# A Mamba block and two windowed-attention layers on one core: packed step products, token shift by transfers, queries rotated on GpSimd, another set-up order

## Chip, cores and metric

The kernel runs on one core of a Trainium2 chip. The metric is device time in microseconds (us) of one execution. Lower is better. Three runs of the kernel before gave a median of 1104.92 us (1102.85 to 1107.98).

## What is computed

The input is 16 sequences of 256 tokens with 128 features. First comes a Mamba block with a layer norm, then two layers of local attention and a gated feed-forward network (FFN), then a second layer norm. Cut to what matters here:

```python
u = silu(causal_conv4(x @ in_w + in_b))                # 256 channels
delta = softplus((u @ dt1_w + dt1_b) @ dt2_w + dt2_b)  # rank 16 in between
h = exp(delta*A)*h + (exp(delta*A)-1)/A * B * u        # 16 states, scan over time
y = (C.h + D*u) * silu(x @ gate_w + gate_b)
x = layernorm(x + y @ out_w + out_b)
x0 = x                                                 # then, for each of 2 layers
q, k, v = split(shift_token(x) @ wqkv)                 # 8 heads of 64
q, k = rotary_xpos(l2norm(q)*qs, l2norm(k)*ks)
x = x + local_attention(8*q, k, v) @ wo                # windows of 64, own and one before
h = layernorm(shift_token(x))*ln_g + ln_b              # shift: features 64.. come from the token before
a, g = split(h @ w1 + b1);  x = x + (a*gelu(g)) @ w2 + b2
out = layernorm(x0 + x)                                # after both layers
```

## The kernel before

Everything is float32, but for the mask. The 16 sequences form ten groups of one or two sequences (`SIZES`, line 27). A group goes through the Mamba block as a whole; `f` numbers the 20 pairs of layer and group (`QUAD`, line 81), and `q` the 64 tiles of 128 tokens within them (`TILE`, line 83). Each engine runs one list of steps written out by hand (`PE_ORDER` to `SP_ORDER`, lines 86 to 357), and `run` issues them in that order; semaphores join the engines. An engine so waits at the head of its list, and all behind it waits too. The groups of the Mamba block run interleaved with the attention and FFN of groups before them.

The steps that matter here:

- **Mamba, group g.** TensorE `rank` (two products of 128 rows x 16 columns over all tokens of the group), ScalarE `rank` (adds the bias), TensorE `step_in` (two products of 17 rows x 128 columns, the 17th row of the input being ones for the bias), ScalarE `softplus` (absolute value, exp, ln), VectorE `step_size` (delta). Then for each of 16 states: ScalarE `decay`, VectorE `scan` (line 1073, both inputs in SBUF), TensorE `state_y` (four quadrants of 64 x 64).
- **Attention, tile q.** TensorE `qk_in` fills both AA banks. ScalarE `squares` and VectorE `sums` give the sums of squares (`ss`), GpSimd `scale` turns them into inverse norms (`rn`: line 756, then a power, line 761). VectorE `rope` (lines 1147 and 1148) multiplies queries and keys by the two rotary tables, into `qkc` and `qks`. For keys GpSimd `rotate` adds the two (line 780) and multiplies by the norm (line 783) into `kr`. For queries TensorE does the sum: `qk_T` transposes `qkc` and `qks` into the same bank (line 1407), and transposes `kr` (line 1413): 24 transposes a tile. The queries' norm is left to the softmax: VectorE `row_max`, GpSimd `exp_bias` (line 774: maximum times norm, `nbias`), ScalarE `softmax` (line 926: eight exponentials with a per-partition bias and scale). GpSimd `inverse` (line 767) gives the inverse row sums.
- **FFN, f.** VectorE `attn_sum` (x2), TensorE `shift`: products of x2 with the identity, a shift matrix and a carry matrix into bank M, five products for every two tiles; VectorE `ffn_stats` and `ffn_norm` read bank M. GpSimd `residual` waits for `ffn_norm`. M stays held until `ffn_norm` is done (`HELD`).
- **Set-up.** ScalarE's queue issues ten loads before the first activation, VectorE clears buffers, convolves group 0, makes the coefficients, casts the mask and scales the rotary tables (`masks`, `rotation_tables`), and only then starts its list.

TensorE's products go through the helper at line 1257; a float32 product shows as two instructions in the trace, a transpose as one.

## Time and profile before

| | |
|---|---|
| median of three runs | 1104.92 us |
| the profiled execution | 1106.03 us, its span 1103.8 us |
| TensorE matmul busy | 967.1 us (88%) |
| VectorE busy | 863.2 us (78%) |
| ScalarE busy | 832.3 us (75%) |
| GpSimd busy | 671.5 us (61%) |
| chain that ended last | PE 47%, ACT 18%, issue 13%, DVE 11%, POOL 11% |

Engine names in the profile: PE is TensorE (PEld its weight loads), DVE VectorE, ACT ScalarE, POOL GpSimd, SP the engine that issues transfers. Busy time is the union of an engine's instructions. A group's busy time is the union of that group's alone, and consecutive matmuls overlap in the records, so groups that alternate add up to more than the engine spends; for what a stretch of TensorE work really takes, the chain is the view to read.

### The profile page before, as it was taken

The numbers are of one execution on the slowest core, as the hardware profiler recorded it, in microseconds if no ns is written. First come the engines' busy times: TensorE is split into PE (matmuls) and PEld (weight loads), VectorE is DVE, ScalarE is ACT, GpSimd is POOL, SyncE is SP. The second block draws the span as 40 slices with busy tenths as digits, with TensorE's granted clock in tenths as the row PEclk, the third lists the DMA queues.
The fourth block names the chain that finished last, engine by engine and source line by source line (L and its number), as shares of the span: only waits on it lengthen the run. The fifth ranks groups of instructions, "written<-read, shape, count | busy, mean of one in ns | idle before, by whom it ended". The sixth has DMA issues, their size and how long they took to land.

```text
span 1103.8 us, 27452 instructions
## 1 busy us (share of the span) xinstructions
PE 967.1 (88%) x10784; PEld 593.9 (54%) x10784; DVE 863.2 (78%) x1184; ACT 832.3 (75%) x1909; POOL 671.5 (61%) x513
## 2 busy tenths in 40 slices
PE   4677779799999899999999999998999999996775
PEld 1222345456555465557465646465665766665463
DVE  7776897898888877998799878996988875642543
ACT  4455777886998669886988699877879887783570
POOL 2004764688578666876567857685656777661561
PEclk9988899899999999999999999999999999998897
DMA  6000100000000100000000110010001011010010
GB/s 217 10 15 1 26 1 15 14 18 15 16 16 17 39 20 16 21 16 19 22 17 16 35 26 15 12 40 10 21 7 30 16 25 26 7 25 6 14 32 10
DMA packets 22354, 25.59 MB, mean 23 GB/s; under 512 B 2710, under 2 KB 14545, under 8 KB 22225
## 3 DMA queue, kind: packets, MB, share of 16 engines
q1 hardware_dynamic: 20783, 22.49, 7.9%
q8 instruction: 86, 1.41, 0.5%
q10 hardware_dynamic: 1442, 1.34, 0.4%
q14 instruction: 43, 0.35, 0.1%
HBM read 9.13 MB, written 2.10 MB: 10 GB/s over the span
## 4 chain that ended last, share of the span: by engine, by line
PE 47%; ACT 18%; issue 13%; DVE 11%; POOL 11%; ACTq 1%; POOLq 0%; DVEq 0%
PE M L1257 11%; PE YY L1257 10%; ACT prob L926 8%; PE AA L1257 8%; PE C L1257 6%; DVE scan L1073 4%; PE BB L1257 4%; POOL rn L761 4%; PE BB L1407 2%; PE BB L1395 2%; POOL rden L767 2%; PE C L1458 1%; ACT qkT L914 1%; ACT probT L895 1%; POOL kr L780 1%
## 5 line engine op out<-in xcount | busy, mean ns | idle before, releaser
L1073 DVE TENSOR_TENSOR_SCAN scan<-du,decay 128x1028 f32<-128x1028 f32 (+1 forms) x160 | 297.4, 1898 | 8.7 <-PE YY L1257 4.9
L926 ACT ACTIVATE prob<-BB,nbias,rn 128x128 f32<-128x128 f32 x472 | 208.7, 464 | 48.0 <-POOL nbias L774 47.3
L761 POOL TENSOR_TENSOR rn<-ssc,expo 128x16 f32<-128x16 f32 x64 | 212.5, 3321 | 19.8 <-ACT prob L926 15.1
L871 ACT ACTIVATE decay<-delta,negA 128x1024 f32<-128x1024 f32 (+1 forms) x160 | 153.3, 985 | 16.6 <-DVE scan L1073 12.1
L767 POOL TENSOR_TENSOR rden<-den,minus 128x8 f32<-128x8 f32 x64 | 126.5, 1976 | 49.5 <-ACT prob L926 49.5
L1257 PE MATMUL YY<-scan,diag 64*64 64x512 f32 (+1 forms) x1280 | 142.7, 538 | 15.3 <-DVE scan L1073 15.2
L1257 PE MATMUL AA<-wqkv,hT 128*128 128x512 f32 x256 | 131.4, 638 | 11.8 <-DVE qks L1148 10.2
L756 POOL TENSOR_SCALAR ssc<-ss 128x16 f32<-128x16 f32 x64 | 47.7, 745 | 91.1 <-DVE ss L1130 90.2
L1130 DVE TENSOR_REDUCE ss<-sq 128x16 f32<-128x1024 f32 x64 | 77.3, 1208 | 29.4 <-ACT sq L889 29.3
L926 ACT ACTIVATION_READ_ACCUMULATOR prob<-BB,nbias,rn 128x1 f32 x472 | 99.8, 211 | 0.0
L1162 DVE TENSOR_REDUCE nmax<-BB 128x8 f32<-128x1024 f32 x59 | 71.9, 1218 | 31.8 <-PE BB L1257 31.6
L889 ACT ACTIVATE sq<-AA 128x512 f32<-128x512 f32 x128 | 71.3, 605 | 22.7 <-PE AA L1257 22.5
L780 POOL TENSOR_TENSOR kr<-qkc,qks 128x512 f32<-128x512 f32 x64 | 84.7, 1323 | 5.9 <-DVE qks L1148 5.9
L914 ACT ACTIVATE qkT<-BB 128x512 f32<-128x512 f32 x118 | 64.2, 599 | 26.3 <-PE BB L1413 26.1
L1147 DVE TENSOR_TENSOR qkc<-AA,rope_c 128x1024 f32<-128x1024 f32 x64 | 77.7, 1214 | 5.2 <-PE AA L1257 2.4
L783 POOL TENSOR_TENSOR kr<-kr,rn 128x512 f32<-128x512 f32 x64 | 77.5, 1211 | 5.0
L1257 PEld LDWEIGHTS AA<-wqkv,hT 128*128 128x128 f32 x256 | 46.6, 199 | 62.7 <-issue 61.6
L1257 PE MATMUL M<-hnT,w 128*128 128x512 f32 (+3 forms) x160 | 71.9, 531 | 8.6 <-ACT hid L952 5.1
L1257 PEld LDWEIGHTS C<-v_even,probT 128*64 128x64 f32 x1024 | 64.5, 138 | 26.9 <-issue 18.7
L1148 DVE TENSOR_TENSOR qks<-AA,rope_s 128x1024 f32<-128x1024 f32 x64 | 77.6, 1213 | 0.0
L895 ACT ACTIVATE probT<-BB 128x1024 f32<-128x1024 f32 x59 | 60.8, 1030 | 22.2 <-PE BB L1395 20.9
L1257 PE MATMUL C<-v_even,probT 128*64 128x64 f32 x1024 | 73.1, 225 | 4.1 <-ACT v_odd L905 2.2
(158 smaller groups left out, 2062.4 us busy)
## 6 DMA issues: line engine op xcount, KB each, us to landing
v_even<-v_odd SPq DMA_DIRECT2D x96, 128.0 KB, 2.3
x<-in_x SPq DMA_DIRECT2D x6, 256.0 KB, 3.8
wqkv<-in_wqkv SPq DMA_DIRECT2D x1, 1536.0 KB
xT<-in_xT SPq DMA_DIRECT2D x6, 256.0 KB, 3.8
out<-outb SPq DMA_DIRECT2D x6, 256.0 KB, 2.6
w<-in_w SPq DMA_DIRECT2D x1, 682.0 KB
xT<-in_xT SPq DMA_DIRECT2D x4, 128.0 KB, 2.6
x<-in_x SPq DMA_DIRECT2D x4, 128.0 KB, 4.4
```

Source lines behind the costliest of these rows:

```text
L761: pool.tensor_tensor(rn[:, q % 2, :], ssc[:, :], expo[:, 0:2 * HEADS], ALU.pow).then_inc(rn_sb, 1)
L767: pool.tensor_tensor(rden[:, q % 2, :], den[:, q % 2, :], minus[:, :], ALU.pow).then_inc(rden_sb, 1)
L780: pool.tensor_tensor(kr[:, :], qkc[:, q % 2, 1, :], qks[:, q % 2, 1, :], ALU.add).then_inc(rope_add, 1)
L783: pool.tensor_tensor(heads(kr[:, :]), heads(kr[:, :]), rn[:, q % 2, HEADS:].unsqueeze(2).to_broadcast((P, HEADS, DH)), ALU.mult).then_inc( ...
L871: act.activation(decay[:, at % A_RING, both(g), 1:], delta[:, both(g), :], ACT.Exp, scale=negA[:, n:n + 1]).then_inc(decay_sb, 1)
L914: act.activation(qkT[:, :, :, lo:lo + WIN], bank_of(q, r)[:, :].rearrange("p (a c x) -> p a c x", a=2, c=PAIRS), ACT.Copy).then_inc(qkT_sb, 1)
L926: ins = act.activation(prob[:, h, :], bank_of(q, a)[:, c * P:(c + 1) * P], ACT.Exp, bias=nbias[:, q % 2, h:h + 1], scale=rn[:, q % 2, h:h ...
L1073: dve.tensor_tensor_scan(state, step, a, 0.0, ALU.add, ALU.mult).then_inc(scan_sb, 1)
L1130: dve.tensor_reduce(ss[:, :], sq[:, :, :].rearrange("p a (h x) -> p (a h) x", x=DH), AX.X, ALU.add).then_inc(ss_sb, 1)
L1147: dve.tensor_tensor(dst_c, src, cos, ALU.mult)
L1148: dve.tensor_tensor(dst_s, src[:, :, :, ::-1, :], sin, ALU.mult).then_inc(rope_mul, 2)
L1257: return pe.matmul(dst, lhsT, rhs, start=start, stop=stop, skip_group_check=True)
```

## The change

- **Shift by transfers.** `shift` leaves TensorE's list. SP issues three transfers for each f, from x2 to a new buffer `xs`: the upper half of the features one partition on, the carry row of odd tiles, the lower half as it is. `ffn_stats` and `ffn_norm` read `xs`; `residual` waits for the transfers.
- **Packed step products.** `rank` becomes four products of 32 columns each, one for each half of the channels and half of the tokens, in four column strips; the two halves of the channels are not summed but kept as rows, which `step_in` sums, with 64 rows, two row halves side by side into the two banks. ScalarE's step covers 128 partitions and half the columns; the absolute value is one instruction instead of two.
- **Queries as keys.** `rotate` works on queries and keys at once, in place in `qkc` (1024 elements a partition instead of 512). `qk_T` waits for it and does 16 transposes. `exp_bias` is gone; the exponentials take the negated maximum as bias and no scale.
- **Set-up.** Most loads move from ScalarE's queue to SP's, in another order, A_log alone comes first; the coefficients come ahead of the convolution, `masks` and `tables` become steps of VectorE's list (`masks 0` first of all; `tables 0` after `differences 1`), and three clearings move to GpSimd.
- **All five lists are written anew**, with other distances between the steps.

```diff
+masks 0, differences 0, step_size 0, scan 0 0, scan 0 1, scan 0 2, scan 0 3, scan 0 4, scan 0 5, scan 0 6,
+scan 0 7, scan 0 8, scan 0 9, scan 0 10, scan 0 11, scan 0 12, scan 0 13, scan 0 14, scan 0 15, gated 0,
+mamba_sum 0, conv0 1, conv1 1, mamba_norm 0, differences 1, tables 0, step_size 1, scan 1 0, scan 1 1, scan 1 2,
...
+load_xT 1, load_xT 2, v_even 0, v_even 1, load_xT 3, shift 0, v_even 2, v_even 3, shift 1, v_even 4, v_even 5,
+v_even 6, v_even 7, v_even 8, v_even 9, v_even 10, shift 2, load_xT 4, v_even 11, v_even 12, shift 3, v_even 13,
+v_even 14, shift 4, store 0, v_even 15, v_even 16, load_x 4, v_even 17, v_even 18, load_xT 5, shift 5, v_even 19,
...
+shift 18, store 7, shift 19, store 8, store 9"""
...
             load_xT(0)
+            sp.dma_start(pv[:, :], t["pv"]).then_inc(w_cols, 16)
             sp.dma_start(gate_w[:, :], t["gate_w"]).then_inc(w_gate, 16)
+            sp.dma_start(dt1_w[:, :, :], t["dt1_w"].rearrange("(h p) r -> p h r", h=HALF)).then_inc(w_step, 16)
...
+            sp.dma_start(bv[:, NST:], t["bv"][NST:].partition_broadcast(P)).then_inc(w_rows, 16)
             for g in range(X_RING):
                 load_x(g)
+            for dst, src in [(prob[:, 0:4, :], t["mask"]), (rope_c[:, 0], t["rope_c"]), (rope_s[:, 0], t["rope_s"]),
+                             (rope_c[:, 1], t["rope_c"]), (rope_s[:, 1], t["rope_s"])]:
+                sp.dma_start(dst, src).then_inc(w_rope, 16)
...
+            def shift(f):
+
+                n, mid = tiles_of(QUAD[f][1]), D // 2
+                sp.wait_ge(x2_sb, f + 1)
+                if f:
+                    sp.wait_ge(hn_sb, f)
+                else:
+                    sp.wait_ge(zeros_late, 1)
+                sp.dma_start(xs[1:P, 0:n, mid:], x2[0:P - 1, 0:n, mid:]).then_inc(sh_in, 16)
+                sp.dma_start(xs[0:1, 1:n:2, mid:], x2[P - 1:P, 0:n:2, mid:]).then_inc(sh_in, 16)
+                sp.dma_start(xs[:, 0:n, 0:mid], x2[:, 0:n, 0:mid]).then_inc(sh_in, 16)
...
+            pool.memset(qkT[:, :, :, 0:WIN], 0.0)
+            pool.memset(xs[0:1, :, :], 0.0)
+            pool.memset(v_even[:, :, :], 0.0).then_inc(zeros_late, 1)
...
-                    pool.wait_ge(prob_sb, 2 * (q - 1))
...
-            def exp_bias(q):
-                if q >= 2:
-                    pool.wait_ge(prob_sb, 2 * (q - 1))
-                pool.wait_ge(rn_sb, q + 1)
-                pool.wait_ge(max_sb, q + 1)
-                pool.tensor_tensor(nbias[:, q % 2, :], nmax[:, q % 2, :], rn[:, q % 2, 0:HEADS], ALU.mult).then_inc(nmax_sb, 1)
-
             def rotate(q):
                 pool.wait_ge(rope_mul, 2 * q + 2)
-                if q:
-                    pool.wait_ge(qkT_ps, 2 * q)
-                pool.tensor_tensor(kr[:, :], qkc[:, q % 2, 1, :], qks[:, q % 2, 1, :], ALU.add).then_inc(rope_add, 1)
+                both_qk = qkc[:, q % 2].rearrange("p a x -> p (a x)")
+                pool.tensor_tensor(both_qk, both_qk, qks[:, q % 2].rearrange("p a x -> p (a x)"), ALU.add).then_inc(rope_add, 1)
                 pool.wait_ge(rope_add, q + 1)
                 pool.wait_ge(rn_sb, q + 1)
-                pool.tensor_tensor(heads(kr[:, :]), heads(kr[:, :]),
-                                   rn[:, q % 2, HEADS:].unsqueeze(2).to_broadcast((P, HEADS, DH)),
+                all_heads = heads(both_qk)
+                pool.tensor_tensor(all_heads, all_heads, rn[:, q % 2, :].unsqueeze(2).to_broadcast((P, 2 * HEADS, DH)),
                                    ALU.mult).then_inc(qk_sb, 1)
...
             def residual(f):
                 l, g = QUAD[f]
-                pool.wait_ge(hn_sb, f + 1)
+                pool.wait_ge(sh_in, SHIFT * (f + 1))
                 rows = x2[:, 0:tiles_of(g), :]
...
+            act.dma_start(in_w[:, :], t["in_w"]).then_inc(w_first, 16)
+            act.dma_start(bv[:, 0:NST], t["bv"][0:NST].partition_broadcast(P)).then_inc(w_rates, 16)
+            load_table(EXP_AND_LN)
+            act.wait_ge(w_rates, 16)
+            act.activation(negA[:, :], bv[:, BV["A_log"]:BV["A_log"] + NST], ACT.Exp).then_inc(a_exp, 1)
+            load_table(SILU)
             act.wait_ge(zeros_ready, 1)
-            act.activation(tack[:, :], zero[:, :], ACT.Exp)
...
-                act.activation(dt1_s[0:RANK, 0:tok_of(g)], Y[0][0:RANK, 0:tok_of(g)], ACT.Identity, bias=col("dt1_b", 0, RANK)).then_inc(d1_sb, 1)
+                n = tok_of(g) // 2
+                act.wait_ge(d1_ps, 2 * HALF * (g + 1))
+                act.activation(dt1_s[:, 0:n], Y[0][:, 0:n], ACT.Identity, bias=col("dt1_b")).then_inc(d1_sb, 1)
...
-                    act.activation(th[:, ab(g, h), :], seqs(bk(Y[h], g)), ACT.Abs).then_inc(za_sb, 1)
-                act.wait_ge(za_sb, HALF * g + HALF)
+                act.wait_ge(z_ps, 2 * HALF * (g + 1))
+                act.activation(by_half(th[:, both(g), :]), z_of(g), ACT.Abs).then_inc(za_sb, 1)
+                act.wait_ge(za_sb, g + 1)
                 act.activation(th[:, both(g), :], th[:, both(g), :], ACT.Exp, scale=-1.0).then_inc(e_sb, 1)
...
-                act.wait_ge(nmax_sb, q + 1)
...
                         h = 2 * c + a
                         ins = act.activation(prob[:, h, :], bank_of(q, a)[:, c * P:(c + 1) * P], ACT.Exp,
-                                             bias=nbias[:, q % 2, h:h + 1], scale=rn[:, q % 2, h:h + 1],
+                                             bias=nmax[:, q % 2, h:h + 1],
                                              accum_out=den[:, q % 2, h:h + 1])
...
-            dve.memset(qkT[:, :, :, 0:WIN], 0.0)
-            dve.memset(v_even[:, :, :], 0.0).then_inc(zeros_ready, 1)
-            dve.wait_ge(w_first, F_W)
+            dve.memset(upre[:, :, 0:TAPS - 1], 0.0).then_inc(zeros_ready, 1)
...
+            def state_weights():
+
+                dve.wait_ge(w_cols, 16)
...
                 dve.engine_nop().then_inc(coeff_done, 1)
 
-            def masks():
+            def masks(_):
                 dve.wait_ge(w_rope, R_W)
                 dve.wait_ge(w_mamba, M_W)
                 dve.tensor_copy(identb[:, :], ident[:, :])
                 dve.tensor_copy(mask[:, :, :, :].rearrange("p j w x -> p (j w) x"), prob[:, 0:4, :]).then_inc(mask_done, 1)
...
-                for h in range(HALF):
-                    ins = dve.scalar_tensor_tensor(out=delta[:, ab(g, h), :], in0=seqs(bk(Y[h], g)), scalar=0.0,
-                                                   in1=th[:, ab(g, h), :], op0=ALU.max, op1=ALU.add)
+                for k in range(2):
+                    ins = dve.scalar_tensor_tensor(out=by_half(delta[:, both(g), :])[:, :, k], in0=z_of(g)[:, :, k], scalar=0.0,
+                                                   in1=by_half(th[:, both(g), :])[:, :, k], op0=ALU.max, op1=ALU.add)
...
-                    dve.wait_ge(nmax_sb, q - 1)
+                    dve.wait_ge(prob_sb, 2 * (q - 1))
...
+                dve.wait_ge(sh_in, SHIFT * (f + 1))
                 for i in range(tiles_of(g)):
-                    ins = dve.bn_stats(f_st[:, i, :], rows[:, i, :])
+                    ins = dve.bn_stats(f_st[:, i, :], xs[:, i, :])
...
+            coefficients()
+            dve.wait_ge(w_cols, 16)
             convolve(0, 0)
             convolve(0, 1)
-            coefficients()
-            masks()
-            rotation_tables()
+            state_weights()
...
-                for h in range(HALF):
-                    ins = mm(Y[0][0:RANK, 0:tok_of(g)], dt1_w[:, h, :], u[:, ab(g, h), 1:], h == 0, h == HALF - 1)
-                ins.then_inc(d1_ps, 1)
+                n = tok_of(g) // 2
+                for k in range(2):
+                    for h in range(HALF):
+                        lo = (2 * k + h) * PART
+                        if SIZES[g] == 2:
+                            rhs = u[:, h * SIZES[g] + k, 1:]
+                        else:
+                            rhs = u[:, h, 1 + k * n:1 + (k + 1) * n]
+                        mm(Y[0][lo:lo + PART, 0:n], dt1_w[:, h, :], rhs).then_inc(d1_ps, 1)
...
                 for h in range(HALF):
-                    mm(bk(Y[h], g), dt2_w[:, h * P:(h + 1) * P], bk(dt1_s, g)).then_inc(z_ps, 1)
+                    for k in range(2):
+                        mm(Y[k][:, h * n:(h + 1) * n], dt2_w[half(k), h * P:(h + 1) * P], dt1_s[half(k), 0:n]).then_inc(z_ps, 1)
...
-                pe.wait_ge(rope_mul, 2 * q + 2)
-                for part in range(2):
+                pe.wait_ge(qk_sb, q + 1)
+                for a in range(2):
                     for c in range(PAIRS):
                         for w in range(2):
-                            pe.matmul(bank_of(q, w)[:, c * WIN:(c + 1) * WIN], (qkc, qks)[part][half(w), q % 2, 0, c * P:(c + 1) * P],
-                                      ident[half(w), half(w)], start=part == 0 and c == 0, stop=part == 1,
-                                      is_transpose=True, skip_group_check=True)
-                pe.wait_ge(qk_sb, q + 1)
-                for c in range(PAIRS):
-                    for w in range(2):
-                        ins = pe.matmul(bank_of(q, w)[:, (PAIRS + c) * WIN:(PAIRS + c + 1) * WIN],
-                                        kr[half(w), c * P:(c + 1) * P], ident[half(w), half(w)], start=False, stop=True,
-                                        is_transpose=True, skip_group_check=True)
-                        if c == PAIRS - 1:
-                            ins.then_inc(qkT_ps, 1)
+                            ins = pe.transpose(bank_of(q, w)[:, (a * PAIRS + c) * WIN:(a * PAIRS + c + 1) * WIN],
+                                               qkc[half(w), q % 2, a, c * P:(c + 1) * P], ident[half(w), half(w)])
+                            if a and c == PAIRS - 1:
+                                ins.then_inc(qkT_ps, 1)
...
-            def shifted(f):
-                l, g = QUAD[f]
-                pe.wait_ge(x2_sb, f + 1)
-                free("shift", f)
-                for i in range(tiles_of(g)):
-                    lo, mid, hi = i * D, i * D + D // 2, (i + 1) * D
-                    mm(M[:, lo:mid], ident[:, :], x2[:, i, 0:D // 2])
-                    ins = mm(M[:, mid:hi], shift[:, :], x2[:, i, D // 2:], True, i % 2 == 0)
-                    if i % 2:
-                        ins = mm(M[:, mid:hi], carry[:, :], x2[:, i - 1, D // 2:], False, True)
-                ins.then_inc(sh_ps, 1)
...
+    dt1_w[:, :RANK] = m["dt1_w"]
+    dt2_w = np.zeros((P, DI), np.float32)
+    for k in (0, P // 2):
+        dt1_b[k:k + RANK, 0] = m["dt1_b"]
+        dt1_b[k + RANK, 0] = 1.0
+        dt2_w[k:k + RANK] = m["dt2_w"]
+        dt2_w[k + RANK] = m["dt2_b"]
+        dt2_w[k + PART:k + PART + RANK] = m["dt2_w"]
```

## Rows read from the trace of the kernel before

**Rows 1.** Windows: stretch; busy us of PE, PEld, DVE, ACT, POOL; PEclk, DMA share, GB/s.

```profile
200.00:950.00 750.00, 711.27 (x8309) 444.36 (x8306) 636.35 (x822) 623.59 (x1449) 523.34 (x384) 0.99 0.08 20
400.00:500.00 100.00, 96.02 (x1068) 56.66 (x1067) 89.74 (x94) 89.63 (x200) 74.57 (x51) 1.00 0.08 20
1000.00:1050.00 50.00, 37.69 (x290) 22.99 (x289) 21.85 (x36) 20.94 (x47) 19.46 (x17) 0.86 0.07 17
```

**Rows 2.** The chain in order of time (start, us, what), a TensorE-bound part.

```profile
503.95 2.18 PE M L1257 x20
506.13 0.64 PE BB L1407 x16
...
517.14 1.91 PE YY L1257 x4
```

**Rows 3.** Waits: engine, line, releaser, us in total, times, longest.

```profile
ACT prob L926 <- POOL nbias L774: 51.0, 28, 6.7
```

**Rows 4.** Windows of line 783 alone, the middle: its instructions are the tiles.

```profile
200.00:950.00 750.00, 62.76 (x51) 0.99 0.08 20
```

**Rows 5.** Groups by form, ScalarE: busy us, mean ns, idle time before and releaser.

```profile
L871 ACT ACTIVATE decay<-delta,negA 128x1024 f32<-128x1024 f32 x96 | 108.5, 1159 | 2.6 <-DVE scan L1073 1.7 <-DVE delta L1052 0.8
...
L860 ACT ACTIVATE th<-th 128x1024 f32<-128x1024 f32 x6 | 6.3, 1058 | 0.2
```

**Rows 6.** Source lines of GpSimd: ns min/median/max, first and last start.

```profile
L780 POOL TENSOR_TENSOR kr<-qkc,qks x64: 1259/1272/2852, 95.8 to 1057.5; 128x512 f32<-128x512 f32 x64
...
L783 POOL TENSOR_TENSOR kr<-kr,rn x64: 1041/1042/2922, 97.2 to 1058.9; 128x512 f32<-128x512 f32 x64
...
L794 POOL TENSOR_TENSOR x<-x,bv x20: 720/1271/2647, 164.8 to 1087.7; 128x512 f32<-128x512 f32 x12, 128x256 f32<-128x256 f32 x8
```

**Rows 7.** Groups of GpSimd instructions, columns as in rows 5.

```profile
L756 POOL TENSOR_SCALAR ssc<-ss 128x16 f32<-128x16 f32 x64 | 47.7, 745 | 91.1 <-DVE ss L1130 90.2
...
L774 POOL TENSOR_TENSOR nbias<-nmax,rn 128x8 f32<-128x8 f32 x64 | 21.3, 332 | 88.1 <-DVE nmax L1162 83.4 <-ACT prob L926 4.7
...
L734 POOL TENSOR_TENSOR diag<-ident,wsum 128x1088 f32<-128x1088 f32 x2 | 4.2, 2128 | 3.0 <-DVEq L1007 3.0
```

**Rows 8.** Timeline (start, us, engine): three scans and GpSimd beside them.

```profile
487.25 6.67 DVE L1073 TENSOR_TENSOR_SCAN scan<-du,decay 128x1028 f32<-128x1028 f32 x3
...
488.50 5.46 POOL L756 TENSOR_SCALAR ssc<-ss 128x16 f32<-128x16 f32 x1
```

**Rows 9.** Source line of the scan, starts 499 to 618 us: ns min/median/max.

```profile
L1073 DVE TENSOR_TENSOR_SCAN scan<-du,decay x17: 2269/2287/3309, 499.2 to 618.3; 128x1028 f32<-128x1028 f32 x17
```

**Rows 10.** Groups by form, VectorE: columns as in rows 5.

```profile
L1073 DVE TENSOR_TENSOR_SCAN scan<-du,decay 128x1028 f32<-128x1028 f32 x96 | 222.1, 2346 | 3.1 <-PE YY L1257 2.5 <-ACT decay L871 0.5
```

**Rows 11.** Transfers: KB each, median us from issue to landing.

```profile
v_even<-v_odd SPq DMA_DIRECT2D x96, 128.0 KB, 2.3
...
rope_s<-in_rope_s ACTq DMA_DIRECT2D x2, 128.0 KB, 8.2
```

**Rows 12.** Timeline of SP: one issue late in the kernel.

```profile
1056.20 0.46 SPq L708 DMA_DIRECT2D v_even<-v_odd  x1
```

**Rows 13.** Timeline of the set-up, ScalarE and VectorE.

```profile
5.72 1.29 ACTq L814 DMA_DIRECT2D rope_s<-in_rope_s  x1
...
8.44 0.82 ACT L824 ACTIVATE upre<-YY,pv 128x256 f32<-128x256 f32 x2
...
16.72 2.23 DVE L1013 CAST mask<-prob 128x512 bf16<-128x512 f32 x1
...
22.58 0.74 DVE L1052 SCALAR_TENSOR_TENSOR delta<-YY,th 128x256 f32<-128x256 f32 x2
```

**Rows 14.** The chain in order of time: step products of group 1, last shift products.

```profile
52.16 1.90 PE YY L1257 x4
54.60 2.08 PE YY L1257 x4
...
1083.60 1.31 PE M L1257 x10
```

More of the change, by code:

```diff
@@ L171 @@
-shift 18, probs_T 62, weighted 62, norm_T 18, out_T 62, probs_T 63, up_gate 18, weighted 63, up_a 18 0,
-up_a 18 1, up_a 18 2, out_T 63, down 18, attn_out 19, shift 19, norm_T 19, up_gate 19, up_a 19 0, up_a 19 1,
-up_a 19 2, down 19"""
+state_y 1 14, state_y 1 15, mamba_out 1, u_in 2, gate_in 2, rank 2, step_in 2, qk_in 1, layer_T 0 1, qk_T 0,
+scores 0, qk_in 2, qk_T 1, qk_in 3, probs_T 0, scores 1, v_in 2, weighted 0, skip 2, state_y 2 0, state_y 2 1,
+probs_T 1, out_T 0, state_y 2 2, qk_T 2, v_in 3, state_y 2 3, weighted 1, scores 2, state_y 2 4, out_T 1,
@@ new lines @@
+attn_out 0, state_y 2 5, state_y 2 6, probs_T 2, qk_T 3, weighted 2, state_y 2 7, scores 3, state_y 2 8,
+state_y 2 9, state_y 2 10, state_y 2 11, state_y 2 12, norm_T 0, up_gate 0, state_y 2 13, state_y 2 14,
+probs_T 3, state_y 2 15, up_a 0 0, out_T 2, mamba_out 2, weighted 3, u_in 3, up_a 0 1, out_T 3, layer_T 0 2,
+gate_in 3, v_in 4, qk_in 4, rank 3, up_a 0 2, step_in 3, qk_in 5, down 0, attn_out 1, qk_T 4, qk_in 6, scores 4,
+layer_T 1 0, v_in 5, qk_in 7, qk_T 5, skip 3, probs_T 4, v_in 6, scores 5, weighted 4, state_y 3 0, state_y 3 1,
```

584 lines of the change are left out of this document (276 added, 308 removed).

## Prediction

> **What bounds the kernel now.** I read the busy shares by windows first. From 200 to 950 us TensorE is busy 711.3 of 750 us (94.8%), VectorE 636.4, ScalarE 623.6, GpSimd 523.3 [rows 1]. The chain in order of time says the same: long unbroken runs of PE pieces, so there the order of TensorE's own work sets the pace [rows 2]. The ends are different: from 1000 us TensorE is busy 75% of the time at a granted clock of 0.86 [rows 1], and the chain goes from engine to engine, piece by piece; the first 160 us are like that too. Last the waits: ScalarE stands 51 us for `nbias`, which GpSimd makes in list order after VectorE's maximum [rows 3]. So three questions: what TensorE's middle loses in work, what engine is next, and what the ends gain or lose in latency.
>
> **TensorE, the middle.** The 51 tiles of the middle [rows 4] are the unit. The shift products of four tiles take 2.18 us of the chain, 0.55 us a tile: 28 us. (The groups of the page count alternating matmuls twice, so I take chain pieces.) The second eight transposes for queries are half of a 0.64 us piece, 0.32 us a tile: 16 us [rows 2]. The step products: a pair of 512-column products takes 1.91 us [rows 2]; `rank` streams a quarter of the columns if its four strips run side by side, `step_in` half, so about 1.4 and 0.95 us a group, and six groups, one of them small, fall in the middle: 12 us. No row shows four 32-column strips; the bounds are no gain (strips one after the other stream as many columns as now) and the quarter, and between them I take the quarter, since in `state_y` four quadrants already run together. The Trainium skill, "TensorEngine Tiling (Array Packing)", section Theoretical Speedup, gives up to 4x for a dimension of at most 32; by it the sum would be the one I take, 655; by the rows' other end, without overlap in `rank`, 663. Sum: 711 - 56 = 655 us.
>
> **ScalarE.** An activation with a per-partition scale over 1024 elements takes 1159 ns, one with a constant scale 1058 [rows 5]: 101 ns for the scale operand. Eight exponentials a tile lose it: 0.8 us a tile, 41 us in the middle, so 583. Bounds: nothing (the operand's fetch hides behind the neighbour) and 0.1 us each; I take the rows' difference, since it does not depend on the size much. The absolute value as one instruction and the shorter bias step save under 1 us a group.
>
> **GpSimd.** The added addition and product are as wide again. An addition takes 720 ns at 256 elements and 1271 at 512 [rows 6], so 2.37 us at 1024; a product 1041 at 512 [rows 6] and 2128 at 1088 [rows 7], so 2.01 us at 1024. `rotate` goes from 2.30 to 4.38 us, 2.08 us more a tile: 106 us. `exp_bias` gives back 332 ns a tile [rows 7], 17 us. Sum 523 + 106 - 17 = 612 us.
>
> **The two SBUF readers.** A tiny GpSimd instruction, 242 to 255 ns when free, took 5.46 us while VectorE ran three scans back to back, and ended with them [rows 8]; over the kernel its mean is 745 ns [rows 7]. It also goes the other way: a scan beside GpSimd work took 3309 ns instead of 2269 [rows 9], and the mask's cast took 2.23 us while GpSimd made its product of 2.13 us [rows 7, 13]. So scans and GpSimd's reads exclude each other, and the longer `rotate` holds longer. A VectorE instruction that meets it waits for the remainder: chance and remainder both grow with the length, so a loss now of about 76 ns a scan (mean 2346 [rows 10] over the minimum, some 7 us over the kernel) grows by (2.37/1.26)^2 = 3.5; I put 12 us on VectorE's middle (648) and 15 on GpSimd's (627). The Trainium skill, "SBUF — State Buffer", section Who interferes with whom, states it as an exclusive lock: a VectorE instruction with two SBUF inputs and a GpSimd instruction that reads SBUF shut each other out for the whole instruction. By that rule, the trace agrees (5.46 us); it is the rule that speaks against this change, since it moves work from TensorE, which never meets the scans, to the engine that does. The rival below is built on it.
>
> **What the middle comes to.** The four sums are 655, 648, 583 and 627: 2513 us of work where it was 2495. What falls is the peak, not the work. Two ends from rows: if TensorE stays the pace at 94.8%, 655/0.948 = 691 us, 59 less; if the four engines together are kept only as busy as now (3.33 engines on the mean), 2513/3.33 = 755, 5 more. The densest stretch here, 400 to 500 us, keeps 3.50 engines busy [rows 1], which would give 718. I take 720: TensorE at 91%, VectorE at 90, GpSimd at 87, ScalarE at 81. **Middle: 30 us less.** In the new lists `qk_T` stands on the mean 22.0 steps behind its `qk_in` (21.5 before, not counting `shift`), and `norm_T` 15.2 behind `attn_out` (12.3): room was made for the transfers, little for the longer `rotate`, which moves qk_T by 2.1 us in a tile's 14.7.
>
> **The transfers.** Each f issues three. SP's copies inside SBUF land in 2.3 us [rows 11] and an issue takes 0.46 us [rows 12], so the last of three lands 3.2 us after x2 at best, about 4 with 256-byte pieces in the same queue, against 2.18 (four tiles) or 1.31 us (two) of products [rows 2, 14]. In the middle the wider distance covers it; bank M is also free earlier, since nothing holds it from `attn_sum` to `ffn_norm`. Behind a waiting `shift` on SP stand `v_even` copies; `weighted` waits for them; I put nothing on it and up to 0.5 us a tile at the upper end. `residual` now waits for transfers instead of `ffn_norm`, with `inverse` and `scale` behind it: landing comes before the norm, so no cost.
>
> **Set-up and first groups.** ScalarE's first activation stands at 8.44 us, behind ten issues, the last from 5.72 to 7.01 us, and a table load [rows 13]; now about 6.4, when `u_in` is through. From the mask's cast at 16.72 us to delta 0 at 22.58 VectorE does mask and rotary tables [rows 13], 5.9 us; the tables leave that way, as `tables 0` they stand where VectorE waits for ScalarE's softplus anyway. Against it: `masks 0` is first in VectorE's list and waits for the rotary loads, now issued on SP behind some twelve others, at about 8 to 9 us instead of 5.72; landing took 8.2 us [rows 11, 13]. That puts the mask at 14 to 17 us, with `differences 0` and `step_size 0` behind it, and delta 0 at 17 to 19: 5 us earlier (bounds 3 and 7; a price for the clearings moved to GpSimd is inside, since its first real input comes later). Step products of groups 1 and 2 lie on the chain: 1.90 to 0.5, 2.08 to 1.05 [rows 14], 3 us together. The first tiles, still unhidden, pay 2 us for `rotate`. **Set-up: 6 us less.**
>
> **The end.** Last f: 1.31 us of products [rows 14] become 3.4, 2.1 more; the one before it shares its wait with the last tiles, 1 more. Four last tiles pay 2.1 us each on GpSimd; from 1000 to 1050 us it is busy 19.5 of 50 us [rows 1], so most of the 8 us fall into its waits: 2.5 more. Five softmaxes on the chain are 0.8 us shorter and lose a GpSimd hop: 5 less. **End: 1 us more.**
>
> Together -6 - 30 + 1 = -35 us. The profiled execution took 1106.0 us (span 1103.8 and 2.2 around it), 1.1 above the median of the runs; so 1071 for it and **1070** for the median.
>
> **Rivals.**
> 1. *TensorE keeps the pace* at 94.8%: middle 59 less, 1041. For it: 400 to 500 us has TensorE at 96% with two others at 90% [rows 1]. Against: GpSimd would be at 91%, where it was at 75.
> 2. *The relief is eaten.* Four nearly equal engines in fixed lists wait for each other; the middle stays at 3.33 busy engines, 755 us; with the ends 1105. A lower clock would work the same way: the granted clock is 0.99 where TensorE is busy 95% and 0.86 where it is 75% [rows 1], and 91% lies between.
> 3. *Slower: the scans shut GpSimd out.* There are 160 scans for 64 tiles, often in runs of two or three. If `rotate`'s two instructions wait w us more a tile than now, the middle is (627 + 51 w)/0.948; from w = 1.65 it is over 750. With w = 2.2, less than half of the 5.2 us that the tiny instruction lost in rows 8, it is 780: 30 more, 1130. Against it: the mean loss of that instruction is only 0.5 us.
> 4. *The packing doesn't overlap*: 8 us more work on TensorE, 8 us in the middle, 1078; it is inside the forecast's own range.
>
> **Chances.** The forecast with rival 4, 0.52 (1055 to 1088); rival 1, 0.17 (1036 to 1055); rival 2, 0.16 (1088 to 1110); rival 3, 0.15. A measurement of this kernel tells about 0.5% from no change, 5.5 us. Faster by more than that: all of the first two and a third of rival 2, 0.74; the same 0.10; slower 0.16. The range leaves out most of rival 3 and a little below rival 1: 1038 to 1112.
>
> **What would show it.** Right: `rotate`'s instructions at 2.4 and 2.0 us; exponentials near 360 ns; TensorE's busy time near 895 us in all; TensorE and VectorE both near 90% in the middle; delta 0 at 17 to 19 us. Wrong: waits of TensorE for line 783's result in many tiles (rival 3), scans with a mean over 2450 ns, waits of VectorE for `xs`, or a clock under 0.95 in the middle (rival 2).

## The result, and the profile after

The changed kernel takes **1165.9 us** (median of 4 runs, 1157.4 to 1168.1) where the kernel before took 1104.5 (4 runs beside it): ratio 1.054, interval 1.048 to 1.060. It is slower by 61 us; the forecast was 1070 with an upper end of 1112, so even the sign is wrong. The profiled execution took 1168.1 us, with a span of 1166.3 us at a mean granted clock of 0.919 (before 0.967).

The page of the kernel after, busy time and the clock by slices:

```profile
PE 939.5 (81%) x10032; PEld 558.8 (48%) x10032; DVE 881.9 (76%) x1180; ACT 786.0 (67%) x1896; POOL 810.4 (69%) x452
PEclk9897899899989999998989998998999897987985
```

The windows of the kernel after (stretch; busy us of PE, PEld, DVE, ACT, POOL; clock, DMA share, GB/s), to be held against [rows 1]:

```profile
200.00:950.00 750.00, 654.29 (x7258) 390.46 (x7256) 631.87 (x783) 557.32 (x1359) 611.78 (x314) 0.95 0.09 23
400.00:500.00 100.00, 85.34 (x876) 48.28 (x874) 84.12 (x108) 78.23 (x179) 81.15 (x44) 0.97 0.09 22
1000.00:1050.00 50.00, 40.05 (x523) 29.43 (x521) 21.77 (x45) 33.51 (x99) 33.93 (x25) 0.90 0.10 23
```

The work went where it was meant to go: over the kernel TensorE has 28 us less than before (967.1 then), ScalarE 46 less, GpSimd 139 more. But no engine is the bound of the middle any more: TensorE is at 87%, VectorE at 84, GpSimd at 82. The clock has gone from 0.99 to 0.95, and the same 750 us hold 47 tiles where they held 51 [rows 4]; the windows of line 797 alone, the product of `rotate`, one instruction a tile (stretch; GpSimd's busy us in it; clock, DMA share, GB/s):

```profile
200.00:950.00 750.00, 111.14 (x47) 0.95 0.09 23
```

Time is lost in waits. The first view to read for that is SyncE's own timeline (start, us, engine, line):

```profile
520.00 0.74 SPq L726 DMA_DIRECT2D xs<-x  x1
520.78 6.49 SPq L727 DMA_DIRECT2D xs<-x  x1
527.32 0.68 SPq L728 DMA_DIRECT2D xs<-x  x1
528.04 0.62 SPq L667 DMA_DIRECT2D xT<-in_xT  x1
```

and line 727 in all (the issue behind the first transfer; ns min/median/max, first and last start):

```profile
L727 SPq DMA_DIRECT2D xs<-x x20: 2645/6431/6530, 133.6 to 1139.6; - x20
```

Line 726 issues the transfer of partitions 0 to 126. The next issue, of a transfer with two pieces, holds SyncE for 6.4 us where f has four tiles and for 2.65 where it has two; I had reckoned 0.46 us an issue [rows 12]. The chain of the kernel after goes straight through it (start, us, what):

```profile
519.31 0.67 DVE x L1186
520.00 0.74 SPq L726
520.78 6.49 SPq L727
527.32 0.68 SPq L728
528.04 3.45 DMA xT<-in_xT
531.54 3.78 PE YY L1264 x4
```

Here even the load of the next group's xT, with which the shift has nothing to do, stands behind it, and TensorE behind that. The chain of the whole kernel by engines, from its page:

```profile
PE 40%; ACT 15%; DVE 12%; issue 10%; SPq 9%; POOL 5%; DMA 4%; DVEq 0%; POOLq 0%; ACTq 0%
```

SyncE has 9% of it and transfers 4%; in the stretch of [rows 2] neither appears. The waits (engine, line, releaser, us in total, times, longest):

```profile
DVE f_st L1192 <- DMA xs<-x: 79.5, 20, 8.8
PE YY L1264 <- DMA xT<-in_xT: 22.2, 5, 6.6
POOL f_ve L763 <- DVE f_mv L1197: 109.7, 16, 23.3
PE M L1485 <- DVE hn L1206: 29.7, 6, 9.0
```

All twenty `ffn_stats` wait for the transfers, 4 us each, with VectorE's scans queued behind them, and GpSimd's `ffn_rstd`, ScalarE's `norm_T` and TensorE's `norm_T` in a row behind those.

### The profile page after: what moved, and what is told of

Its sections match the earlier page's. It is cut to its first block, busy times and chain, and to the rows that moved or that the text cites. A ratio compares the mean times of both kernels' runs of the same rounds, so it can differ in the third digit from the quotient of the medians.

```text
span 1166.3 us, 25804 instructions
## 1 busy us (share of the span) xinstructions
PE 939.5 (81%) x10032; PEld 558.8 (48%) x10032; DVE 881.9 (76%) x1180; ACT 786.0 (67%) x1896; POOL 810.4 (69%) x452
## 4 chain that ended last, share of the span: by engine, by line
PE 40%; ACT 15%; DVE 12%; issue 10%; SPq 9%; POOL 5%; DMA 4%; DVEq 0%; POOLq 0%; ACTq 0%
PE M L1264 9%; PE YY L1264 8%; PE AA L1264 7%; SPq L727 7%; PE C L1264 7%; DVE scan L1082 4%; ACT prob L934 4%; PE BB L1264 3%; DMA xs<-x 3%; PE BB L1421 2%; PE C L1467 2%; POOL rn L782 2%; PE BB L1409 1%; ACT decay L879 1%; DVE qks L1157 1%
## 5 line engine op out<-in xcount | busy, mean ns | idle before, releaser
L1082 DVE TENSOR_TENSOR_SCAN scan<-du,decay 128x1028 f32<-128x1028 f32 (+1 forms) x160 | 315.9, 2017 | 12.4 <-PE YY L1264 7.8
L782 POOL TENSOR_TENSOR rn<-ssc,expo 128x16 f32<-128x16 f32 x64 | 224.3, 3504 | 5.3
L934 ACT ACTIVATE prob<-BB,nmax 128x128 f32<-128x128 f32 x472 | 166.1, 380 | 51.0 <-DVE nmax L1171 50.6
L793 POOL TENSOR_TENSOR qkc<-qkc,qks 128x1024 f32<-128x1024 f32 x64 | 158.2, 2472 | 5.3 <-DVE qks L1157 5.2
L797 POOL TENSOR_TENSOR qkc<-qkc,rn 128x1024 f32<-128x1024 f32 x64 | 145.3, 2271 | 5.0
L934 ACT ACTIVATION_READ_ACCUMULATOR prob<-BB,nmax 128x1 f32 x472 | 103.9, 220 | 0.0
L763 POOL TENSOR_SCALAR f_ve<-f_mv 128x4 f32<-128x4 f32 (+1 forms) x20 | 11.1, 553 | 110.0 <-DVE f_mv L1197 109.7
L1264 PE MATMUL M<-hnT,w 128*128 128x512 f32 (+3 forms) x160 | 77.5, 569 | 6.4 <-ACT hid L960 4.0
L944 ACT ACTIVATE oT<-C 128x512 f32<-128x512 f32 x64 | 38.7, 605 | 61.2 <-PE C L1467 58.5
L1264 PE MATMUL C<-v_odd,probT 128*64 128x64 f32 x1024 | 78.0, 233 | 0.0
```

The lines of the kernel that those rows point to most:

```text
L782: pool.tensor_tensor(rn[:, q % 2, :], ssc[:, :], expo[:, 0:2 * HEADS], ALU.pow).then_inc(rn_sb, 1)
L793: pool.tensor_tensor(both_qk, both_qk, qks[:, q % 2].rearrange("p a x -> p (a x)"), ALU.add).then_inc(rope_add, 1)
L797: pool.tensor_tensor(all_heads, all_heads, rn[:, q % 2, :].unsqueeze(2).to_broadcast((P, 2 * HEADS, DH)), ALU.mult).then_inc(qk_sb, 1)
L934: ins = act.activation(prob[:, h, :], bank_of(q, a)[:, c * P:(c + 1) * P], ACT.Exp, bias=nmax[:, q % 2, h:h + 1], accum_out=den[:, q % 2, ...
L1082: dve.tensor_tensor_scan(state, step, a, 0.0, ALU.add, ALU.mult).then_inc(scan_sb, 1)
L1264: return pe.matmul(dst, lhsT, rhs, start=start, stop=stop, skip_group_check=True)
```

## The experiments

Every run was timed in three rounds beside the kernel before (medians 1103.8 to 1107.4 us in the four sets); a ratio is always to that. A difference of medians from two sets carries their 3.6 us with it; where it matters, the difference by the ratios stands beside it. "Old order" is the kernel before's lists of steps, "new order" the changed kernel's.

**1. The first transfer in two.** Expected before it ran:

> The changed kernel with one edit: the transfer that moves x2 down by one row (partitions 0-126 to 1-127) is issued as two, of 112 partitions and of 15, so a shift is four transfers. Theory T (the 127-partition transfer is what costs: the second issue of each shift holds SyncE's list 6.4 us for a four-tile f and 2.7 us for a two-tile f, and its bytes land late): every issue of the shift under 1 us, SyncE's share of the chain of waits from 9% to under 3%, VectorE's wait of f_st for the transfer from 79.5 us to under 35 us, TensorE's wait for xT (22.2 us) near nothing; time 1075 to 1110 us. Rival L (lock: GpSimd's rotate of 4.7 us and VectorE's long scans slow each other, mean scan 2524 ns against 2346): the issues get short but the time stays above 1145 us and the scans stay above 2500 ns. Rival O (the new hand-written order is the worse one whatever the transfers cost): above 1140 us with DVE, ACT and PE waiting for each other, not for transfers.

```diff
-sp.dma_start(xs[1:P, 0:n, mid:], x2[0:P - 1, 0:n, mid:]).then_inc(sh_in, 16)
+sp.dma_start(xs[1:CUT + 1, 0:n, mid:], x2[0:CUT, 0:n, mid:]).then_inc(sh_in, 16)
+sp.dma_start(xs[CUT + 1:P, 0:n, mid:], x2[CUT:P - 1, 0:n, mid:]).then_inc(sh_in, 16)
```

(with CUT = 112 and SHIFT = 16 * 4). Measured **1116.3 us**, ratio 1.011 (1.007 to 1.015): the same bytes in one more transfer are 50 us faster (47 by the ratios). The issue behind the first transfer is line 728 of this kernel (ns min/median/max):

```profile
L728 SPq DMA_DIRECT2D xs<-x x20: 911/952/1708, 132.1 to 1088.1; - x20
```

and its waits have for VectorE:

```profile
DVE f_st L1194 <- DMA xs<-x: 31.2, 12, 4.4
```

The wait fell by 48 us, the time by 50. Theory T holds, and lock and order (L and O) are refuted as the cause of these 50 us, since both wanted more than 1140 us. Some of T's numbers missed: 1116 is just above the 1075 to 1110 expected, TensorE's wait for xT fell from 22.2 to 7.3 us and not to nothing, and one issue took 1.7 us. Rival L's other mark, scans over 2500 ns, is nearly met (2498), and the kernel is still 12 us over the kernel before; that is left to experiments 5 to 7.

**2 and 3. The size or the number of partitions?** The same kernel with the cut moved to 126 and to 113:

> split_transfer with the cut at 126: one transfer of 126 partitions and one of a single partition. Theory D (a transfer is spread over as many of the 16 DMA engines as divide its number of partitions, at most 16: 14 for 126, 16 for 112, one for 127): the issues behind it stay under 1.2 us and the time is within 1% of split_transfer, 1105 to 1128 us. Rival S (size or lack of a full set of partitions): near the changed kernel's 1166 us, with an issue of some 6 us.

> split_transfer with the cut at 113, a prime: transfers of 113 and 14 partitions, that is one partition more and one less than in split_transfer. Theory D: the issue behind the first is held 113/127 of 6.4 us for a four-tile f, some 5.7 us, and most of the gain of the split is gone, 1148 to 1168 us. Rival S (the size alone): issues under 1.2 us and 1105 to 1128 us.

```diff
-        CUT = 112
+        CUT = 126
```

and CUT = 113. Measured **1116.5 us** (ratio 1.009, 1.007 to 1.011) for 126 and **1167.5 us** (1.057, 1.052 to 1.061) for 113. The issue behind the first transfer, with 126 partitions in it:

```profile
L728 SPq DMA_DIRECT2D xs<-x x20: 632/663/676, 133.8 to 1089.9; - x20
```

and with 113:

```profile
L728 SPq DMA_DIRECT2D xs<-x x20: 2276/5656/5738, 132.4 to 1140.0; - x20
```

One partition more than 112 costs 51 us; with 126, thirteen more again, they are back. So size is refuted (rival S) and theory D stands. For 113 and 127, both primes, the hold scales with the pieces: 5656/6431 is 0.88, and 113/127 is 0.89. The two sizes of f agree: 508 pieces of 256 bytes hold the issue 3786 ns longer than 254 (6431 against 2645), and 452 hold it 3380 ns longer than 226 (5656 against 2276), 14.9 and 15.0 ns for each piece more. The windows tell how many engines moved the bytes: the last two figures are the mean busy share of the core's 16 DMA engines and GB/s. While the first transfer runs, in the kernel after and in cut_113:

```profile
521.00:527.00 6.00, 4.63 (x40) 3.23 (x38) 1.90 (x4) 4.79 (x20) 5.92 (x4) 1.00 0.07 16
520.50:525.50 5.00, 4.15 (x39) 3.04 (x37) 1.42 (x3) 4.00 (x18) 4.92 (x4) 1.00 0.08 17
```

and in split_transfer (112 partitions, then 15) and cut_126:

```profile
501.10:501.60 0.50, 0.50 (x2) 0.23 (x2) 0.50 (x1) 0.50 (x4) 0.50 (x1) 1.00 0.90 188
502.00:502.20 0.20, 0.20 (x1) 0.00 (x1) 0.20 (x1) 0.20 (x2) 0.20 (x1) 1.00 0.39 72
509.20:509.70 0.50, 0.50 (x2) 0.00 (x1) 0.50 (x2) 0.50 (x4) 0.50 (x2) 1.00 0.88 192
```

A share of 0.07 to 0.08 is little more than one engine of 16, at 16 to 17 GB/s; 0.9 is nearly all of them, at 190. And 15 partitions reach 0.39, over six engines, so it is not that 127 and 113 are odd. That is the rule of the Trainium skill, "DMA: Bandwidth & Descriptors", section Why a DMA increments its semaphore by 16 and not by 1: the number of DMA engines that share a transfer is the largest one up to 16 that divides its slowest dimension, so 16 for 112 or 128 partitions and one for 127; by it 126 has 14 and 113 one. The times agree in all four cases, and the shares with one engine for 127 and 113; 16 for 112 against 14 for 126 is more than shares of 0.90 and 0.88 can tell apart.

**4. Held list or late bytes?** The changed kernel, unsplit, with the three transfers issued the other way round:

> The changed kernel, unsplit, with the three transfers of a shift issued in the opposite order, so that the 127-partition one comes last. Rival H (SyncE's list held 6.4 us is the loss): the first two issues at 0.7 us, what follows is held only where it comes within 6 us, time 1125 to 1145 us. Theory W (what costs is that VectorE waits for the late bytes): f_st's wait stays near 75 us and the time within 1% of the changed kernel's, 1152 to 1178 us.

```diff
-sp.dma_start(xs[1:P, 0:n, mid:], x2[0:P - 1, 0:n, mid:]).then_inc(sh_in, 16)
-sp.dma_start(xs[0:1, 1:n:2, mid:], x2[P - 1:P, 0:n:2, mid:]).then_inc(sh_in, 16)
 sp.dma_start(xs[:, 0:n, 0:mid], x2[:, 0:n, 0:mid]).then_inc(sh_in, 16)
+sp.dma_start(xs[0:1, 1:n:2, mid:], x2[P - 1:P, 0:n:2, mid:]).then_inc(sh_in, 16)
+sp.dma_start(xs[1:P, 0:n, mid:], x2[0:P - 1, 0:n, mid:]).then_inc(sh_in, 16)
```

Measured **1180.6 us** (1.067, 1.066 to 1.069), 15 us worse than the changed kernel and a little over the top of theory W's range. Its timeline of SyncE:

```profile
524.95 0.72 SPq L728 DMA_DIRECT2D xs<-x  x1
525.72 6.41 SPq L667 DMA_DIRECT2D xT<-in_xT  x1
```

and VectorE's wait:

```profile
DVE f_st L1192 <- DMA xs<-x: 95.9, 20, 9.6
```

All three issues of the shift are now quick; the hold moved on to whatever comes next, here the load of xT. That is so behind 15 of the 20 long transfers: the next load or `v_even` copy takes 2.6 to 6.5 us. VectorE's wait grew from 79.5 to 95.9 us, 0.8 us for each of the twenty: the long transfer starts two issues later. Rival H's 1125 to 1145 us did not come, and issuing the long transfer last gains nothing. But the list was not free in this run either, and TensorE still waits 20.4 us for xT (22.2 in the kernel after). So whether the late bytes or the held list make more of the 50 us is not shown; that the wait of `ffn_stats` for the bytes fell by 48 us with the split speaks for the bytes.

**5 to 7. What split transfers and the rotation still cost.** Three kernels on top of split_transfer, in the new order, which leave work out:

> split_transfer with GpSimd's rotation cut to the half of the keys (512 elements a partition in place of 1024), same order, waits and everything else; the queries go on without their sum and their norm, so the output differs from the reference's. It prices the doubled rotation in the new order with nothing given back. Theory G (GpSimd's longer list costs even in the new order): 1065 to 1100 us, against 1116. Rival (the rotation is hidden there, the rest of the gap is TensorE and the transfers): 1108 us or more.

> split_transfer without any shift: ffn_stats and ffn_norm read x2 itself, no transfers, no TensorE; the residual goes to the buffer that the transfers filled. The output differs from the reference's. It gives the time with a shift that costs nothing, so the difference to split_transfer is all that split transfers still cost. Theory T2 (the landing of 3 us plus about 3 us of issues, twenty times, 31 us of f_st's waits, partly hidden): 1085 to 1105 us. Rival (split transfers are free): 1112 us or more.

> split_no_shift and split_half_rotate together (output differs from the reference's). If the two costs are of their own, the gains add; if both wait in one chain it is more or less than the sum. Theory: 1045 to 1080 us, near the forecast's 1070, which counted the transfers and the rotation at nothing. If it stays above 1095 us, what is wrong with the forecast is elsewhere (order, TensorE).

```diff
-both_qk = qkc[:, q % 2].rearrange("p a x -> p (a x)")
-pool.tensor_tensor(both_qk, both_qk, qks[:, q % 2].rearrange("p a x -> p (a x)"), ALU.add).then_inc(rope_add, 1)
+keys = qkc[:, q % 2, 1, :]
+pool.tensor_tensor(keys, keys, qks[:, q % 2, 1, :], ALU.add).then_inc(rope_add, 1)
```

for the half rotation (the product likewise), and for no shift:

```diff
-dve.wait_ge(sh_in, SHIFT * (f + 1))
+dve.wait_ge(x2_sb, f + 1)
-    ins = dve.bn_stats(f_st[:, i, :], xs[:, i, :])
+    ins = dve.bn_stats(f_st[:, i, :], x2[:, i, :])
```

| kernel, new order | us | ratio (interval) |
|---|---|---|
| split_transfer | 1116.3 | 1.011 (1.007 to 1.015) |
| split_half_rotate | 1093.8 | 0.986 (0.981 to 0.990) |
| split_no_shift | 1090.2 | 0.982 (0.978 to 0.985) |
| split_neither | 1064.5 | 0.958 (0.954 to 0.963) |

The half rotation alone gives 23 us, no shift alone 26, both 52 (by the ratios 28, 33 and 58): the two costs add, so neither hides the other. And with both gone the kernel stands at 1064, where the forecast had 1070 with both counted at almost nothing. Its windows:

```profile
200.00:950.00 750.00, 693.97 (x8015) 421.68 (x8006) 653.16 (x854) 608.34 (x1512) 553.69 (x352) 0.98 0.09 21
```

TensorE is at 92.5% and the clock at 0.98, as the forecast drew its middle; GpSimd is at 74%, where the forecast had 87 with the whole rotation. With the half rotation GpSimd's share of the chain falls from 17% (split_transfer) to 8%. Part of the rotation's 23 us may go through VectorE. Groups by form, the wide scans (busy us, mean ns, idle time before) in split_transfer:

```profile
L1084 DVE TENSOR_TENSOR_SCAN scan<-du,decay 128x1028 f32<-128x1028 f32 x96 | 236.5, 2498 | 6.9 <-PE YY L1266 5.7 <-ACT decay L881 1.2
```

and in split_half_rotate:

```profile
L1083 DVE TENSOR_TENSOR_SCAN scan<-du,decay 128x1028 f32<-128x1028 f32 x96 | 225.8, 2387 | 6.8 <-PE YY L1265 6.2 <-ACT decay L880 0.6
```

Scans are 11 us shorter over the kernel, and all of VectorE 23 (886.4 against 863.3), though nothing was edited there; GpSimd itself has 134 us less (806.9 against 673.1). Which of the two carries the 23 us of time these runs can't say.

**8 and 9. Each part alone, in the old order.**

> The kernel before with one part of the change alone: the shift by three transfers in place of TensorE (part_b of the skip product lies in hu's room, so that xs fits), everything else and the order of all other steps as before. Theory T: the whole loss comes from here, 1145 to 1180 us, the second issue at 6.4 us for a four-tile f. Rival L: no more than 1115 us, since rotate is the old one. Rival O: no more than 1115 us, since the order is the old one.

> The kernel before with the other part alone: the sums and norms of queries on GpSimd beside those of keys, 16 transposes a tile in place of 24, exponentials without a scale operand, no exp_bias step; shift on TensorE, order as before. Theory T: within 1.5% of before, 1085 to 1110 us; TensorE's busy time down by about 20 us, exponentials near 380 ns, rotate at 2.4 + 2.2 us. Rival L: slower, 1125 us or more, with scans above 2500 ns. Rival O: as T.

The edits are those of the diff, cut to one part, in the kernel before. Transfers alone, unsplit: **1228.8 us**, 1.113 (1.108 to 1.118), 49 over the top of what T expected. The rotation alone: **1164.1 us**, 1.055 (1.051 to 1.059): T expected no more than 1110, and rival L, 1125 or more, had it right in time. Exponentials (382 ns) and `rotate` (2.49 and 2.21 us) came as T said; TensorE's busy time did not fall by 20 us but rose from 967.1 to 971.5, at a clock of 0.944. The chain of before_plus_rotate by engines:

```profile
POOL 40%; PE 25%; issue 19%; DVE 9%; ACT 5%; ACTq 1%; DMA 0%; POOLq 0%; DVEq 0%; SPq 0%
```

and TensorE's wait for the rotated queries and keys:

```profile
PE BB L1387 <- POOL qkc L764: 41.1, 21, 4.9
```

The chain of the kernel before had 11% GpSimd. Rival L wanted scans over 2500 ns; they are at 2460 here, and 2346 before [rows 10]. So the lock falls short of what L asked of it, and GpSimd's list has the larger part by the chain: with 611 us busy in the middle (81.5%) in an order made for 523, it is what the others wait for. No run separates the two. GpSimd's share had room; the order had none.

**10. All but the transfers, old order.**

> The changed kernel's set-up, packed step products and rotation with the kernel before's shift on TensorE and the kernel before's order of steps. Theory T: 1070 to 1100 us, faster than before, since only the transfers are missing and they were the loss. Rival L: 1125 us or more, since GpSimd's longer rotate is in it. Rival O: no more than 1105 us, and split_transfer stays above 1140.

Edit: the changed kernel with `shifted` and its matrices back on TensorE and the lists of before. Measured **1152.2 us** (1.042, 1.038 to 1.047). T is wrong here too: without the transfers it is not the gain that is left but the rotation's loss, 12 us smaller than in before_plus_rotate, by packing and set-up.

**11 to 13. The order.**

> split_transfer with the kernel before's order of steps on all engines. Beside all_but_transfers (1152) it tells what split transfers cost in that order, beside split_transfer (1116) what the order is worth. Theory G: the order is worth 35 us or more, since the new one was made for the longer rotate: 1150 to 1185 us. If the order doesn't matter: 1110 to 1125 us.

> split_transfer with the rotation as before the change: keys alone on GpSimd, 24 transposes a tile, exponentials with scale, exp_bias back (put where row_max ended in split_transfer's trace). So the new order, split transfers, packed step products and new set-up are left. Theory G (GpSimd's doubled rotate puts its list on the chain: 40% of the chain in before_plus_rotate): GpSimd out of the chain (under 12%), mean wait for ssc unchanged, 1080 to 1105 us. Rival O2 (the new order is the cost, the rotation is well placed in it): 1115 us or more, because TensorE has 8 transposes and ScalarE 100 ns an exponential more to do than split_transfer.

> The changed kernel with the shift back on TensorE in the new order (shift put up to four steps ahead of norm_T, ffn_stats of six of the 20 moved back on VectorE to fit). Theory T: the transfers were the loss, so this is 1085 to 1120 us, as good as split_transfer (1116) or better, since an x2 is there for ffn_stats after some 1.5 us of TensorE and not after 5. Rival B (TensorE bound: 28 us of it come back and end on the path): 1130 us or more.

| order | parts | us | ratio (interval) |
|---|---|---|---|
| old | all parts, transfers split | 1210.6 | 1.096 (1.094 to 1.098) |
| new | all parts, transfers split | 1116.3 | 1.011 (1.007 to 1.015) |
| new | the same, rotation as before | 1166.4 | 1.057 (1.054 to 1.060) |
| new | all parts, shift on TensorE | 1164.5 | 1.055 (1.053 to 1.057) |

The new order is worth 94 us to the new parts; 35 or more had been expected, and 1150 to 1185 us for the old order, so theory G has the direction and not the size. In the old order split transfers cost 58 us (1210.6 against 1152.2) and the rotation 60. But in the new order, to put either of the two back as it was costs about 50 us as well; what was expected of both (T's 1085 to 1120, G's 1080 to 1105) failed, and rivals B and O2 were right in time. (GpSimd's share of the chain, under 12% by G, is 13%.) The chain of split_queries_back by engines:

```profile
PE 32%; ACT 23%; issue 16%; POOL 13%; DVE 8%; SPq 1%; DMA 1%; POOLq 0%; ACTq 0%; DVEq 0%
```

ScalarE has 23% of it, where split_transfer had 10%. It waits for the step put back in, `exp_bias`:

```profile
POOL nbias L809 <- DVE nmax L1193: 90.4, 34, 11.4
ACT prob L956 <- POOL nbias L809: 69.4, 37, 5.8
```

I placed `exp_bias` and `shift` by the trace of split_transfer; an order made for them could do better. So these two runs don't price their parts. They show that a part's price can't be read apart from the order.

**14 and 15. The parts that bring something.**

> The kernel before with the packed step products alone (rank and step_in in quarters and halves, one Abs in place of two, merged max). By the forecast's sum TensorE has about 12 us less in the middle; theory: 1085 to 1105 us, never slower. Rival (packing doesn't overlap, and step_size gets a longer wait, since both halves must be there before the one Abs): 1103 to 1115 us.

> The kernel before with the packed step products and the new order of the set-up, no transfers, rotation and order of steps as before. before_plus_packed was 1101.5 us against 1105.6; all_but_transfers against before_plus_rotate (1152 and 1164) says that packing and set-up together are worth 12 us beside the rotation. Theory: 1090 to 1100 us, faster than both kernels. Rival (set-up's gain is taken back by the first groups' waits): 1100 to 1108 us.

The edits are the diff's parts for `rank`, `step_in`, the one absolute value and the two maxima in before_plus_packed, and the set-up as well in before_packed_setup; shift, rotation and order as before. Measured **1101.5 us**, 0.996 (0.995 to 0.998), and **1092.8 us**, 0.986 (0.982 to 0.989). The second beats both kernels. Products of the four strips, then of the two halves, in the middle of the kernel after (timeline; start, us):

```profile
427.46 0.64 PE L1264 MATMUL YY<-u,dt_w 128*32 128x256 f32 x8 [0.56 <-ACT u L847]
434.96 1.14 PE L1264 MATMUL YY<-dt_s,dt_w 64*128 64x256 f32 x8
```

and the same two in the kernel before:

```profile
420.65 1.89 PE L1257 MATMUL YY<-u,dt_w 128*16 128x512 f32 x4
428.38 1.98 PE L1257 MATMUL YY<-dt_s,dt_w 17*128 17x512 f32 x4
```

The strips do run side by side: 2.1 us less a group. But TensorE's whole relief of 20 us (967.1 to 947.1 busy) moved the time by only 4. The set-up brings 9 more by the medians and 12 by the ratios.

## Why the prediction was wrong, point by point

**The transfers, the step that failed first.** The sentence "an issue takes 0.46 us [rows 12], so the last of three lands 3.2 us after x2 at best" took SyncE's price from copies of 64 partitions [rows 11, 12] and put it on one of 127. No row of before has a transfer with a prime number of partitions; the term needed a bound of its own, and the 0.5 us a tile at the upper end, 32 us in all, was put on the copies behind the shift and is too small as well. The rule of the Trainium skill named under experiments 2 and 3, which speaks against this transfer, was not weighed. Measured: 6.4 us a hold, 50 us of time for the number 127 alone, and 26 more for the shift by split transfers against one that costs nothing. "In the middle the wider distance covers it" and the 3 us at the end are wrong by 73 us in all.

**GpSimd and the middle.** The durations were near: addition 2472 ns and product 2271 in the kernel after (2.37 and 2.01 forecast). That GpSimd is busy 612 us in the 750, the very sum of the prediction, is chance: they are 612 us for 47 tiles, 13.0 a tile, and the sum had 51 tiles and 12.0, 12.3 with the lock's 15 us. What failed is "TensorE at 91%, VectorE at 90, GpSimd at 87" as a state that the lists would reach. The doubled half of the rotation costs 23 to 26 us even in the order made for it, and some 60 in the old one (1164 against 1104), where the sum had 4.5 for the ends and, beyond 12 and 15 us of busy time for the lock, nothing for the middle. My rival 3 named GpSimd, but by a stretch of `rotate` through scans (w over 1.65 us); `rotate` is at 4.74 us, 0.36 over the forecast's 4.38. The chains point rather to GpSimd's list (40% in before_plus_rotate, 17% in split_transfer against 8% with the half rotation); wide scans at 2524 ns, above the mark of 2450 set for it, say that the lock has a share, whose size stays open. Of the other wrong signs that the text named, VectorE waits for `xs`, and the clock in the middle is at the mark of 0.95; of the right ones only the set-up's came, and the durations nearly.

**The sum.** 1070, less 3 for the transfers and 4.5 for the rotation's ends, is 1062 for a kernel without either; split_neither is 1064. From there the runs lead back to the time measured: 26 for the rotation (split_no_shift, 1090), 26 for a shift by split transfers (1116), 50 for the number 127 (1166). So two terms were mis-sized, and the rest held in total. That 1062 and 1064 lie so close is in part luck: of the terms that can be read alone, the set-up gave 9 to 12 us where 6 was forecast, and packing 4 where its 12 us of work in the middle and 3 us of time at the start were in the sum.

**TensorE.** Forecast 895 us busy, measured 939.5, at a clock of 0.919 where it had been 0.967; in split_neither 914.5 at 0.951. Busy time times the mean granted clock gives an estimate of the work at full clock: 935 us before, 863 after, 870 in split_neither, and 865 for the forecast at the old clock. By that estimate the work fell as forecast, and what is over it in busy time came with the lower clock. The clock was lower where there was more waiting: 0.99 where TensorE is busy 95% [rows 1], 0.95 at 87%, and in the profiled runs as a whole 0.905 in the slowest kernel and 0.97 in before_packed_setup. A split of one transfer brought the mean from 0.919 to 0.940, which is 0.021 of the 0.048 lost; what the lower clock adds to the time of its own was not measured.

**ScalarE.** Exponentials went from 464 to 380 ns, where 360 was forecast: the operand is worth 84 ns, not 101. What this is worth in time no run separates; ScalarE has 15% of the chain in the changed kernel, 18% before.

**Set-up.** Delta 0 starts at 17.53 us (forecast 17 to 19, before 22.58 [rows 13]); the runs of the old order give 9 to 12 us for set-up, against 6. **Packing** overlaps (rival 4 is out), but 20 us less busy time came as 4 us of time.

**"What falls is the peak, not the work."** That was said of the four sums, and it should have been the warning: lowering TensorE by 56 us pays only where TensorE is the last to be ready. In before_plus_packed 20 us less busy time brought 4.

## What to carry to other kernels

Before a copy between partitions is taken as cheap, look at its number of partitions: 15, 112, 126 and 128 were quick here, 113 and 127 held the next issue 6 us each with four tiles, and cutting one transfer in two gave 50 us back. Busy shares say whether an engine has room, not whether its list has: price moved work by the chain through the receiving engine, and measure each part of a bundle by itself, in an order made for it. Here the two small parts of the change are worth 1.4% and the two large ones, as made, are a loss.

## What the runs showed of the hardware

- A transfer inside SBUF over 127 or 113 partitions in pieces of 256 bytes keeps SyncE in its next issue, whatever that is: 6431 ns after 127 x 4 pieces, 2645 after 127 x 2, 5656 after 113 x 4, 2276 after 113 x 2, so 14.9 to 15.0 ns for each piece more. Meanwhile the 16 DMA engines are busy 0.07 to 0.08 and move 16 to 17 GB/s. After 112 or 126 partitions the next issue takes 0.95 and 0.66 us, with shares of 0.90 and 0.88 and some 190 GB/s.
- The hold shows at the issue after the slow one (line 727 and not 726); in long_last it showed at a load of another tensor and at copies.
- VectorE's busy time changed with no edit there: 886.4 to 863.3 us, and its wide scans from 2498 to 2387 ns, when GpSimd's rotation was halved.
- An exponential over 128 elements with bias and scale from SBUF takes 464 ns in the kernel before, with the bias alone 380 ns in the kernel after.
